# Row sums from ScalarE's accumulator, and gate work spread over four rounds, in a two-layer attention and expert kernel

## The chip, the cores and the metric

The kernel runs on one core of one Trainium2 chip. The metric is the device time of one execution in microseconds (us). Engines: TensorE (PE; its weight loads are PEld), VectorE (DVE), ScalarE (ACT), GpSimd (POOL) and SyncE (SP), each with an instruction stream of its own, synchronized by semaphores.

## What is computed

Two layers over x (16 batches, 128 rows, 128 columns, float32). Each layer adds a cross attention and a mixture of experts to x. The parts that matter here are the second attention and the first layer's gate:

```
x = x + attention_0(layernorm(x), ctx)
l = layernorm(x) @ gate_w.T                 # 8 experts
top_val, top_idx = top_k(l, 2);  w = softmax(top_val)
x = x + sum_e w_e * (layernorm(x) @ We[e])  # the two best experts of each row
q, k, v from layernorm(x) and ctx, 16 heads of 64
p     = softmax(q k / 8) over the first 124 context rows
p_ipa = softmax(q k / 8) over the last 4 context rows
x = x + ((p v + p_ipa v) @ Wo + ...)
x = x + experts_1(layernorm(x))             # 16 experts choose their rows
```

## The kernel before, in words

All engines run hand-written, software-pipelined rounds, one for each batch b. After the first attention's rounds (`round0`) come the second attention's (`round1`, b from -1 to 16), and then the second layer's experts. The work of one batch is spread over several rounds. In round b of `round1`:

- PE makes the scores of batch b (L1490, `scores`, two halves of 16 matmuls), transposes the powers of batch t = b - 1 (L1501, `turn`), makes queries (L1510), keys (L1518) and values (L1538) of batch f = b + 1, the outputs of t (L1531), the first layer's expert products of batch g = b + 4 (L1443, `ffn`, two halves in bank 7), and the projection of t (L1700).
- DVE, for each of four groups of four heads: `shifted` (L759 to L762) takes the maxima of the scores, `turned` (L770) copies transposed powers out of PSUM, `summed` (L776, L778) adds up the 124 powers of each head, in one reduction for four heads, and takes the reciprocal. It also does half of the scaling of the expert products (L732), the softmax over the last 4 context rows (`ipa_norm`, L783 to L787), the residual (L306), statistics (L310, L572, L575) and normalized inputs (L301).
- ACT: `powers` (L1130) makes the exponentials, one instruction for each head, 128x124, with the head's negated maximum as bias; `queries`, `outputs`, `values` and the key copy (L1137, L1143, L1148, L1237) bring results out of PSUM; `weighted` (L1092) scales four expert products.
- POOL: `norm` (L498) multiplies four heads' powers with the reciprocals, `experts_sum` (L481, L483) adds the eight scaled expert products of g, `rstds` (L432) gives the power -1/2 of variances.

The **gate work** is done for four batches at a time, j = 0 to 3 (group j is batches 4j to 4j + 3). Its parts are `head_input` (DVE, L698: four normalized inputs), `head_turn` (PE, L1431), `head_turned` (ACT, L1079), `head_logits` (PE, L1438, then three steps on DVE, L705 to L707), `head_powers` (ACT, L1084) and `head_weights` (DVE, nine steps, L713 to L725: ties and beats over all pairs of experts, 128x256 elements, the count, and the shares). Each of the twelve DVE steps adds one to the semaphore F.step, and DVE waits for it before the next; ACT's `weighted` waits for the twelfth of its group. `head_of(b)` says in which round a group is done: j = 1 in round -1, 2 in round 3, 3 in round 7. Groups 2 and 3 take their inputs at the ends of rounds 2 and 6 (`if b in (2, 6)`), and their weights at the ends of rounds 3 and 7, behind `ipa_norm` and ahead of the residual. Group 2 is first used by `weighted` in round 4, group 3 in round 8.

The order on each engine is the order of the calls in `round1`; nothing is reordered. In round b, PE waits for the residual of t - 1 (Z.x_new) before it writes bank 7 again, and for the first copied block of t (Z.p_sb) before the second half of the queries. The transposes of t wait for POOL's `norm` of t and for `ipa_norm`.

```
if j:
    head_turn(j, bank[7])
...
if there(g):
    if j:
        pe.wait_ge(F.step, HEAD_STEPS * j + 1)
    ffn(g, 0, bank[7])
```

## Time and profile before

| | |
|---|---|
| time, median of 3 runs | 526.05 us (525.59 to 528.3) |
| the profiled execution's own time | 526.27 us |
| its span, first to last instruction | 524.5 us |
| granted TensorE clock, mean | 0.998 of full |
| PE, PEld busy | 494.0, 380.1 us |
| DVE, ACT, POOL busy | 396.8, 271.6, 235.3 us |

A row of a timeline gives the start, the time until the last of its instructions ends, engine, line of the kernel, operation, out<-in, shapes and count (xN: so many instructions in one row); in brackets the idle time of the engine just before and who ended it. Instructions of one engine can overlap, so that a next row may start a little before the end of the one ahead. A row of the table by stretch gives the length and each engine's busy time in it.

### The profile page before, as it was taken

How to read it: one execution, taken by the hardware profiler on the slowest of the kernel's cores; microseconds unless marked ns; L12 is line 12 of the kernel's file. 1: busy time of each engine (PE TensorE's matmuls, PEld its weight loads, DVE VectorE, ACT ScalarE, POOL GpSimd, SP SyncE). 2: the span in 40 equal slices, each digit the busy share in tenths (PEclk: the TensorE clock that was granted, in tenths of full speed). 3: DMA queues.
4: the chain of work that ended last, by engine and by line, in shares of the span. 5: the costliest groups of instructions: out<-in, count | busy, mean ns of one | idle time of the engine just before them, and what ended most of it. 6: DMA issues, size and time to landing. Idle time of an engine off the chain costs nothing.

```text
span 524.5 us, 13371 instructions
## 1 busy us (share of the span) xinstructions
PE 494.0 (94%) x5109; PEld 380.1 (72%) x5113; DVE 396.8 (76%) x1064; ACT 271.6 (52%) x728; POOL 235.3 (45%) x331
## 2 busy tenths in 40 slices
PE   4799999999999998999989999999989999999996
PEld 3566666656667776777767777788757897799995
DVE  5888989766797889777897879778986678536553
ACT  3366565445666565564745575564663544513332
POOL 5845454044365542675245653533321890080540
PEclk9999999999999999999999999999999999999999
DMA  8900000000001110111000000022200300001001
GB/s 229 224 4 3 2 2 3 4 1 7 4 1 32 32 34 0 32 32 33 2 1 2 4 2 1 3 63 62 55 10 19 104 0 2 0 4 41 2 2 41
DMA packets 21872, 14.47 MB, mean 28 GB/s; under 512 B 5929, under 2 KB 21137, under 8 KB 21809
## 3 DMA queue, kind: packets, MB, share of 16 engines
q1 hardware_dynamic: 20704, 13.31, 9.7%
q8 instruction: 42, 0.69, 0.6%
q10 hardware_dynamic: 1104, 0.30, 0.3%
q14 instruction: 22, 0.17, 0.1%
HBM read 12.30 MB, written 1.05 MB: 25 GB/s over the span
## 4 chain that ended last, share of the span: by engine, by line
PE 74%; DVE 18%; issue 3%; ACT 2%; DMA 1%; POOL 1%; ACTq 0%; DVEq 0%; POOLq 0%
PE bank L1771 9%; PE bank L1780 5%; PE bank L1531 5%; PE bank L1443 5%; PE bank L1354 5%; PE bank L1538 4%; PE bank L1518 4%; PE bank L1700 4%; PE bank L1490 4%; PE bank L1510 4%; PE bank L1501 3%; PE bank L1787 3%; PE bank L1589 3%; PE bank L1339 3%; DVE negmax L760 2%
## 5 line engine op out<-in xcount | busy, mean ns | idle before, releaser
L498 POOL TENSOR_TENSOR work<-work,rsum 128x496 f32<-128x496 f32 x64 | 64.1, 1014 | 131.7 <-DVE rsum L778 131.7
L1130 ACT ACTIVATE work<-bank,negmax 128x124 f32<-128x124 f32 x256 | 72.5, 376 | 77.7 <-DVE ipa_s L762 77.7
L533 POOL TENSOR_SCALAR work<-work,slot 128x128 f32<-128x128 f32 x64 | 49.6, 792 | 48.3 <-DVE slot L853 29.4
L1771 PE MATMUL bank<-work 128*128 128x256 f32 x224 | 53.4, 381 | 0.0
L995 DVE SCALAR_TENSOR_TENSOR work<-work,bank 128x256 f32<-128x256 f32 x64 | 26.9, 420 | 33.0 <-ACT work L1282 32.8
L481 POOL TENSOR_TENSOR work<-work 128x512 f32<-128x512 f32 (+2 forms) x48 | 40.2, 838 | 12.1 <-DVE work L732 9.6
L1282 ACT ACTIVATE work<-bank 128x256 f32<-128x256 f32 x64 | 24.5, 383 | 40.6 <-PE bank L1771 29.1
L1771 PEld LDWEIGHTS bank<-work 128*128 128x128 f32 x224 | 40.3, 190 | 4.7 <-DVE work L998 0.2
L760 DVE TENSOR_REDUCE negmax<-bank 128x4 f32<-128x496 f32 x64 | 42.3, 661 | 0.0
L776 DVE TENSOR_REDUCE sums<-work 128x4 f32<-128x496 f32 x64 | 41.4, 647 | 0.5 <-ACT work L1130 0.5
L629 DVE TENSOR_REDUCE negmax<-bank 128x8 bf16<-128x1024 f32 x32 | 39.1, 1220 | 3.1 <-PE bank L1324 2.5
L432 POOL TENSOR_TENSOR rstd<-veps,minus_half 128x1 f32<-128x1 f32 (+3 forms) x28 | 21.0, 752 | 45.3 <-DVE veps L575 45.2
L1510 PE MATMUL bank<-xT,work 128*128 128x128 f32 x256 | 34.6, 279 | 7.0 <-DVE x_all L306 4.1
L770 DVE COPY work<-bank 128x512 f32<-128x512 f32 x60 | 40.7, 678 | 0.8 <-PE bank L1501 0.8
L1490 PEld LDWEIGHTS bank<-work 64*128 64x128 f32 x512 | 31.1, 187 | 13.9 <-issue 8.9
L1501 PE MATMUL bank<-ident,work 128*128 128x128 f32 x256 | 40.1, 279 | 0.3 <-DVE work L787 0.3
L1490 PE MATMUL bank<-work 64*128 64x128 f32 x512 | 37.2, 285 | 1.0 <-issue 1.0
L1510 PEld LDWEIGHTS bank<-xT,work 128*128 128x128 f32 x256 | 31.1, 192 | 9.4 <-issue 4.7
L1071 ACT ACTIVATE work<-bank 128x1024 f32<-128x1024 f32 x32 | 31.0, 1021 | 11.8 <-PE bank L1339 11.8
L1531 PEld LDWEIGHTS bank<-work 128*64 128x64 f32 x512 | 27.4, 136 | 13.3 <-issue 10.4
L1700 PEld LDWEIGHTS bank<-work 128*128 128x128 f32 x256 | 31.0, 191 | 7.4 <-issue 5.1
L1531 PE MATMUL bank<-work 128*64 128x128 f32 x512 | 35.0, 279 | 0.8 <-DVE work L770 0.6
(197 smaller groups left out, 1082.7 us busy)
## 6 DMA issues: line engine op xcount, KB each, us to landing
work<-in_L_ffn_w_dram SPq DMA_DIRECT2D x42, 128.0 KB, 2.4
x_all<-in_x_dram SPq DMA_DIRECT2D x4, 256.0 KB, 5.3
out_dram<-x_all SPq DMA_DIRECT2D x4, 256.0 KB, 2.5
ctx_all<-in_ctx_dram SPq DMA_DIRECT2D x4, 192.0 KB, 5.8
ctx_all<-in_L_ffn_w_dram SPq DMA_DIRECT2D x6, 128.0 KB, 2.3
work<-in_L_xattn_Wq_dram SPq DMA_DIRECT2D x1, 512.0 KB, 6.8
work<-in_L_xattn_Wo_dram SPq DMA_DIRECT2D x1, 512.0 KB, 9.1
work<-in_L_ffn_We_dram SPq DMA_DIRECT2D x1, 512.0 KB, 6.6
```

What stands on the lines that cost most here:

```text
L498: pool.tensor_tensor(part, part, rsum1[:, b % 2, CH * n:CH * n + CH].unsqueeze(2).broadcast_to((128, CH, ORG)), ALU.mult).then_inc(Z.norm, 1)
L533: ins = pool.tensor_scalar(ohw_of(e)[:, k, :], count[:, :], slot[:, h, 0, k, e % E1:e % E1 + 1], slot[:, h, 1, k, e % E1:e % E1 + 1], ALU. ...
L760: dve.tensor_reduce(negmax1[:, b % 2, part], got_s[:, :, 0:ORG], X, ALU.max, negate=True)
L770: dve.tensor_copy(p1T[:, CH * n:CH * n + CH, :], blocks(bank[(4, 6, 5, 4)[n]])).then_inc(Z.p_sb, 1)
L776: dve.tensor_reduce(sums1[:, b % 2, part], p1[:, b % 2, n, :, 0:ORG], X, ALU.add).then_inc(Z.sum, 1)
L1130: ins = act.activation(p1[:, b % 2, n, c, 0:ORG], blocks(bank[n])[:, c, 0:ORG], ACT.Exp, bias=negmax1[:, b % 2, CH * n + c:CH * n + c + 1])
L1490: mm = pe.matmul(blocks(bank[2 * half + odd])[:, c, :], q1T[rows, b % 2, CH * half + c, :], k1T[rows, b % 2, CH * half + c, :], start=True ...
L1501: mm = pe.transpose(blocks(bank[(4, 6, 5, 4)[n]])[:, c, :], p1[:, t % 2, n, c, :], ident[:, :])
L1510: mm = pe.matmul(blocks(bank[5 - n])[:, c, :], wq1[:, part], xT[:, f % 2, :], start=True, stop=True)
L1531: mm = pe.matmul(blocks(bank[5 - n])[D1 * odd:D1 * odd + D1, c, :], v1[:, t % 2, D1 * h:D1 * h + D1], p1T[:, CH * (2 * n + odd) + c, :], s ...
L1700: mm = pe.matmul(bank[7][:, 0:D], o1T[:, c, :], wo1[:, c, :], start=(c == 0), stop=(c == 7))
L1771: mm = pe.matmul(halves(bank[4 + c])[:, n, :], up_weights(e, n, c), xgT[e // E1][:, :, e % E1, :], start=True, stop=True)
```

## The change

ACT's exponentials get an accumulator output, which writes the sum of each head's 124 powers to `sums1`; DVE's reduction L776 and its semaphore go, and `summed` is the reciprocal alone. The gate work of groups 2 and 3 is moved: inputs are taken two at a time at the ends of rounds -1 and 0 (group 2) and 3 and 4 (group 3); transposes and logits are in rounds 1 and 5; the nine steps of the weights are split into `head_ties` (two steps, rounds 2 and 6), `head_beats` (three, rounds 3 and 7) and `head_shares` (four, rounds 4 and 8). Ties and beats stand in front of the third `shifted`, shares in front of `ffn_statistics`. ACT's `head_turned` stands ahead of the first `powers` of its round instead of behind it. PE waits for the input copy xT of batch b + 1 before the gate's transposes.

```diff
--- before.py
+++ after.py
@@ -253,7 +253,7 @@
 
         W = named(sem, "w", "turned downT alpha ctx made taken added")
         Z = named(sem, "z", "xn xb tr xT q q_sb k0 k1 k0_sb k1_sb ki v v_sb vi0 vi1 score ipa_max maxed ipa_exp ipa_step ipa_p "
-                            "exp sum rsum norm turned p_sb p_odd o o_sb proj x_new stats")
+                            "exp rsum norm turned p_sb p_odd o o_sb proj x_new stats")
 
         R = named(sem, "r", "wide count tok picks xn tr xT hid th h logit max ex step topx top turned slot")
         G = named(sem, "g", "told oh got xg")
@@ -295,7 +295,7 @@
 
         def head_of(b):
 
-            return (b + 5) // 4 if (b + 5) % 4 == 0 and b <= 7 else None
+            return {-1: 1, 1: 2, 5: 3}.get(b)
 
         def dve_xn(dve, Z, b, u):
             dve.tensor_scalar(xn[:, u, :], x_all[:, b, :], mv[:, b, 0:1], rstd[:, b, :],
@@ -706,16 +706,23 @@
                 step(dve.tensor_reduce(top0[:, :], lg[:, :, :], X, ALU.max))
                 step(dve.tensor_tensor(ew[:, :, :], lg[:, :, :], top0[:, :].unsqueeze(2).broadcast_to(each), ALU.subtract))
 
-            def head_weights(j):
-
-                mine = lg[:, :, :].unsqueeze(3).broadcast_to(pairs)
-                other = lg[:, :, :].unsqueeze(2).broadcast_to(pairs)
+            mine = lg[:, :, :].unsqueeze(3).broadcast_to(pairs)
+            other = lg[:, :, :].unsqueeze(2).broadcast_to(pairs)
+
+            def head_ties():
+
                 step(dve.tensor_tensor(tie[:, :, :, :], other, mine, ALU.is_ge))
                 step(dve.tensor_tensor(tie[:, :, :, :], tie[:, :, :, :], lower[:, :, :].unsqueeze(1).broadcast_to(pairs),
                                        ALU.mult))
+
+            def head_beats():
+
                 step(dve.tensor_tensor(beat[:, :, :, :], other, mine, ALU.is_gt))
                 step(dve.tensor_tensor(beat[:, :, :, :], beat[:, :, :, :], tie[:, :, :, :], ALU.max))
                 step(dve.tensor_reduce(nbeat[:, :, :], beat[:, :, :, :], X, ALU.add))
+
+            def head_shares(j):
+
                 dve.wait_ge(F.ex, j + 1)
                 step(dve.scalar_tensor_tensor(ew[:, :, :], nbeat[:, :, :], 1.5, ew[:, :, :], ALU.is_lt, ALU.mult))
                 step(dve.tensor_reduce(wsum[:, :], ew[:, :, :], X, ALU.add))
@@ -723,6 +730,12 @@
                 to = ffn_w[:, 4 * (j % 2):4 * (j % 2) + 4, :]
                 after(dve, F.ys0, 4 * (j - 1))
                 step(dve.tensor_tensor(to, ew[:, :, :], wsum[:, :].unsqueeze(2).broadcast_to(each), ALU.mult))
+
+            def head_weights(j):
+
+                head_ties()
+                head_beats()
+                head_shares(j)
 
             def weighted(g, got_y):
 
@@ -773,8 +786,6 @@
 
                 dve.wait_ge(Z.exp, CH * b + n + 1)
                 part = slice(CH * n, CH * n + CH)
-                dve.tensor_reduce(sums1[:, b % 2, part], p1[:, b % 2, n, :, 0:ORG], X, ALU.add).then_inc(Z.sum, 1)
-                dve.wait_ge(Z.sum, CH * b + n + 1)
                 dve.reciprocal(rsum1[:, b % 2, part], sums1[:, b % 2, part]).then_inc(Z.rsum, 1)
 
             def ipa_norm(b):
@@ -883,8 +894,14 @@
                     hidden(1)
                 if b == 14:
                     eight(0, 1)
+                if b in (4, 8):
+                    head_shares((b + 4) // 4)
                 if there(b + 3) and b >= 0:
                     ffn_statistics(b + 3)
+                if b in (2, 6):
+                    head_ties()
+                if b in (3, 7):
+                    head_beats()
                 if there(b):
                     shifted(b, 2)
                 if b == 12:
@@ -921,8 +938,8 @@
                     summed(b, 2)
                     summed(b, 3)
                     ipa_norm(b)
-                if head_of(b):
-                    head_weights(head_of(b))
+                if b == -1:
+                    head_weights(1)
                 if there(b + 3) and b < 0:
                     ffn_statistics(b + 3)
                 if b == 9:
@@ -953,8 +970,10 @@
                     slot_weights(0)
                 if b == 15:
                     rstd_at["half", 2] = variances(Z.stats, B - 1, 12, B - 1)
-                if b in (2, 6):
-                    head_input((b + 6) // 4)
+                if b in (-1, 3):
+                    head_input((b + 9) // 4, 0, 2)
+                if b in (0, 4):
+                    head_input((b + 8) // 4, 2, 4)
                 if there(b + 3):
                     xn1_of(b + 3)
                 if b == -1:
@@ -1127,8 +1146,9 @@
 
                 act.wait_ge(Z.maxed, CH * b + n + 1)
                 for c in range(CH):
+                    h = CH * n + c
                     ins = act.activation(p1[:, b % 2, n, c, 0:ORG], blocks(bank[n])[:, c, 0:ORG], ACT.Exp,
-                                         bias=negmax1[:, b % 2, CH * n + c:CH * n + c + 1])
+                                         bias=negmax1[:, b % 2, h:h + 1], accum_out=sums1[:, b % 2, h:h + 1])
                 ins.then_inc(Z.exp, 1)
 
             def queries(f, n):
@@ -1182,10 +1202,10 @@
 
             def round1(b):
                 f, t, g = b + 1, b - 1, b + 4
+                if head_of(b):
+                    head_turned(head_of(b), bank[7])
                 if there(b):
                     powers(b, 0)
-                if head_of(b):
-                    head_turned(head_of(b), bank[7])
                 if b == 12:
                     route_turned(0)
                 if b == 13:
@@ -1602,6 +1622,7 @@
                     gather(4)
                 after(pe, Z.x_new, t)
                 if j:
+                    after(pe, Z.xT, b + 2)
                     head_turn(j, bank[7])
                 if b == 12:
                     route_turn(0, bank[7])
```

## Rows read from the trace of the kernel before

**Rows 1.** Part 1 of the page: busy time and share of each engine

```profile
PE 494.0 (94%) x5109; PEld 380.1 (72%) x5113; DVE 396.8 (76%) x1064; ACT 271.6 (52%) x728; POOL 235.3 (45%) x331
```

**Rows 2.** Stretches: length, then PE, PEld, DVE, ACT, POOL busy, clock; rounds 1, 3, 4, 5

```profile
145.57:162.05 16.48, 15.86 (x138) 12.25 (x138) 13.37 (x37) 10.30 (x31) 11.31 (x16) 1.00 0.09 26
...
177.62:196.28 18.66, 17.36 (x151) 13.56 (x150) 16.90 (x44) 10.51 (x31) 8.13 (x11) 1.00 0.09 24
196.28:214.80 18.52, 16.07 (x138) 12.27 (x138) 15.16 (x43) 9.69 (x29) 8.20 (x13) 1.00 0.09 24
214.80:230.37 15.57, 15.57 (x138) 12.22 (x137) 12.10 (x35) 9.69 (x29) 7.95 (x12) 1.00 0.10 28
```

**Rows 3.** Timeline of PE, rounds 3 and 4

```profile
179.93 0.63 PE L1431 MATMUL bank<-ident,work 128*128 128x128 f32 x4 [0.56 <-DVE work L698]
...
182.62 1.06 PE L1438 MATMUL bank<-work 128*128 128x8 f32 x8 [0.74 <-ACT work L1079]
...
200.06 1.16 PE L1510 MATMUL bank<-xT,work 128*128 128x128 f32 x8 [2.03 <-DVE x_all L306]
```

**Rows 4.** Timeline of DVE, rounds 2 to 4

```profile
178.27 1.51 DVE L698 TENSOR_SCALAR work<-x_all,mv,rstd 128x128 f32<-128x128 f32 x4
...
193.98 1.25 DVE L713 TENSOR_TENSOR work<-work 128x256 f32<-128x256 f32 x1
195.26 1.37 DVE L714 TENSOR_TENSOR work<-work,lower 128x256 f32<-128x256 f32 x1
...
199.71 0.29 DVE L306 TENSOR_TENSOR x_all<-bank,x_all 128x128 f32<-128x128 f32 x1
```

**Rows 5.** Timeline of DVE, round -1

```profile
128.67 0.42 DVE L714 TENSOR_TENSOR work<-work,lower 128x256 f32<-128x256 f32 x1
...
132.74 1.28 DVE L301 TENSOR_SCALAR xn<-x_all,mv,rstd 128x128 f32<-128x128 f32 x1 [0.66 <-POOL rstd L432]
```

**Rows 6.** Timeline of DVE, round 5

```profile
218.69 0.66 DVE L776 TENSOR_REDUCE sums<-work 128x4 f32<-128x496 f32 x1
...
220.75 0.17 DVE L759 TENSOR_REDUCE ipa_max<-bank 128x4 f32<-128x16 f32 x1 [0.62 <-PE bank L1490]
```

**Rows 7.** Timeline of ACT, round 3: the smallest activation

```profile
190.02 0.24 ACT L1084 ACTIVATE work<-work 128x32 f32<-128x32 f32 x1
```

**Rows 8.** All instructions of line L1130: duration ns min/median/max, first and last start

```profile
L1130 ACT ACTIVATE work<-bank,negmax x256: 354/365/474, 137.3 to 388.0; 128x124 f32<-128x124 f32 x128
```

**Rows 9.** Timeline of ACT, round 5

```profile
216.86 1.13 ACT L1130 ACTIVATE work<-bank,negmax 128x124 f32<-128x124 f32 x4 [3.15 <-DVE ipa_s L762]
...
219.80 1.21 ACT L1092 ACTIVATE work<-bank,work 128x128 f32<-128x128 f32 x4
221.62 1.13 ACT L1130 ACTIVATE work<-bank,negmax 128x124 f32<-128x124 f32 x4 [0.61 <-DVE ipa_s L762]
222.97 1.13 ACT L1130 ACTIVATE work<-bank,negmax 128x124 f32<-128x124 f32 x4 [0.21 <-DVE ipa_s L762]
...
224.57 0.60 ACT L1143 ACTIVATE work<-bank 128x512 f32<-128x512 f32 x1 [0.34 <-PE bank L1531]
```

**Rows 10.** Timeline of PE, round 5

```profile
222.48 1.02 PE L1443 MATMUL bank<-work 128*128 128x512 f32 x2
...
226.56 1.12 PE L1538 MATMUL bank<-work,cT_all 96*124 96x512 f32 x2
```

**Rows 11.** Timelines of PE and ACT, round 0

```profile
141.55 1.12 PE L1443 MATMUL bank<-work 128*128 128x512 f32 x2
...
140.29 1.21 ACT L1092 ACTIVATE work<-bank,work 128x128 f32<-128x128 f32 x4
141.31 2.22 ACT L1130 ACTIVATE work<-bank,negmax 128x124 f32<-128x124 f32 x8
```

**Rows 12.** Timeline of PE, rounds 14 and 15

```profile
372.17 1.09 PE L1531 MATMUL bank<-work 128*64 128x128 f32 x16 [0.35 <-DVE work L770]
...
386.50 1.13 PE L1589 MATMUL bank<-work 128*128 128x512 f32 x2 [0.87 <-DVE work L861]
```

## The prediction

> **What bounds the kernel now.** I read the engines' shares first [rows 1]: TensorE (PE) is busy 94% of the span, VectorE (DVE) 76%, ScalarE (ACT) 52%. So time can only come out of places where PE stands still, or in by making it stand. The table by stretch [rows 2] cuts the second attention at the starts of PE's score matmuls. The ordinary round (214.80 to 230.37) takes 15.57 us and PE is busy for all of it: nothing that DVE or ACT saves there moves the time. Round 3 takes 18.66 and round 4 18.52; rounds 7 and 8 repeat them to the hundredth. Those four are 3.09 + 2.95 + 3.09 + 2.95 = 12.08 us above the ordinary round, and that is the sum in play. Round 1 is 0.91 above.
>
> Where the 12.08 goes is in PE's timeline [rows 3]. In round 3 PE waits 0.56 for the four gate inputs, then 0.74 for ACT's copy of their transposes; the gate's own matmuls are four in 0.63 and eight in 1.06, so 0.11 each and 0.2 to fill: twelve and one filling are about 1.4 that PE has to do. This, with the waits and their restarts, is the excess. In round 4 PE waits 2.03 for the residual. DVE's timeline [rows 4] says why: the nine steps of the gate weights run from 193.98 to 199.71 ahead of the residual, 5.7 us, while PE had ended that round's projection at about 196.3. The two-input steps are slow there: L713 took 1.25 and L714 1.37, beside GpSimd's expert sums. The same L714 took 0.42 in round -1, while GpSimd was idle [rows 5].
>
> **The change, part by part.** *Sums.* 64 reductions on DVE go, four a round, 0.66 each [rows 6], spaced 0.68 with the wait: 2.7 us of DVE a round. In an ordinary round they are hidden: DVE waits for PE 0.62 before L759 even so. What is left on DVE is the reciprocal, which now waits for ACT.
>
> *The accumulator on ACT.* The trace has no activation with an accumulator. I count it as one more small instruction behind each of the 16 activations of a round, r each. Nearest row: the 128x32 activation at 0.24 [rows 7]. Four exponentials of 0.365 (the median [rows 8]) take 1.13 together [rows 9], so neighbours overlap by (4 x 0.365 - 1.13) / 3 = 0.11. If the read overlaps like its neighbours, r is 0.24 - 0.11 = 0.13, or 0.09 with so few elements; if it neither overlaps nor lets the next start, r is 0.24 + 0.11 = 0.35. Below zero is excluded, as work is only added. I take 0.13, since every back-to-back pair in the rows overlaps, and keep 0.09 and 0.35 for the range.
>
> The Trainium skill ("ScalarE: Activation LUTs", section on what ACT_TABLE_LOAD costs) gives an activation with immediates 186 ns + 0.833 per element and an overlap of 93: one element would then add 94 ns, an estimate by that page, and the sum below would come out about 0.6 us lower. The page does not price the accumulator's read, and by its own figures an exponential of 124 elements would be spaced 290 ns, where the rows give 255; so I stay with the rows.
>
> What ACT can bear in an ordinary round [rows 9, 10]: the scaled copies L1092 end at 221.01 and PE needs them at 222.48, 1.47 later, with 8 reads ahead: r up to 0.18. The output copy L1143 ends at 225.17 and PE's L1538 starts at 226.56, 1.39 later, with 16 reads ahead, and ACT idled 0.61 + 0.21 + 0.34 before, plus 3 x 0.11 of overlap: 2.88 / 16, again 0.18. So at 0.13 the read is hidden in every ordinary round and costs nothing; above 0.18 it costs up to 16 x (r - 0.18) a round. This is the one threshold of the case.
>
> *Where ACT has no cover: round 0* [rows 11]. PE's second expert matmul starts at 141.55, as ACT's copies end (141.50), so 8 reads delay it by 1.0; the last powers, end 143.5, go back by 16 reads, and with them the key copy behind them, which PE's last value matmul of the round needs. 2.1 us on ACT bound it above, the 1.0 below; I take +1.5 for round 0, in the middle. Round 1's 0.9 of excess came from DVE's reductions ahead of the softmax's rest; they are gone: -0.9.
>
> *The gate inputs.* Four L698 in one place become two and two, at the ends of rounds -1 and 0, and 3 and 4. In round -1 the pair falls into the 0.66 that DVE waits for GpSimd's power before L301 [rows 5]: nothing. Round 0 has no residual to end with. At the end of round 3 it puts 2 x 0.38 [rows 4] ahead of the shift and copy of round 4, for which PE's second query half waits; how much PE has in hand there no row says, so 0 to 0.75, and I take +0.2, since in the ordinary round PE does not wait for that copy at all. At the end of round 4 the next round begins with the gate's matmuls, which cover it.
>
> *Gate matmuls.* They move from rounds 3 and 7 to 1 and 5. PE keeps 2 x 1.4 = +2.8. The inputs are a round old, so the 0.56 goes; ACT now copies the transposes ahead of the first powers, where it idled 3.15 [rows 9], so the 0.74 goes. The powers start about 0.5 later, behind which PE has 1.4 more work of its own.
>
> *Gate weights.* Nine steps, 5.7 us, come out of the end of rounds 3 and 7. Two go in front of the third shift of rounds 2 and 6, three into 3 and 7, four into 4 and 8. Uncontended they take 0.9, 1.3 and 1.1 (0.42 to 0.43 a wide step [rows 5]); GpSimd's first normalization, about 1 us, may hit the first of them: 1.3, 1.7 and 1.1. The place has 0.62 of wait plus the 0.68 of the reduction that left, 1.3. What runs over (0.4) delays the third copy. In round 5 the shift begins at 220.75 [rows 6] and with its copy takes about 1.4, to 222.2; PE comes to the outputs that need it behind L1443, about 223.4 [rows 10]: 1.2 in hand, so 0.4 is hidden. The shares in round 4 end about when ACT reaches the scaled copies that wait for them. So these steps cost nothing as long as the reduction is gone too.
>
> *The added wait* on xT ahead of the transposes is for a copy made a round before: nothing. No DMA moves; SP's queue is untouched.
>
> *Rounds 14 and 15.* DVE holds PE there: 0.35 before L1531 and 0.87 before a gather [rows 12]. The reduction just ahead leaves: -0.5 in round 14. In round 15 DVE gains about 1 but ACT's gathered copies come later by some of the reads: -0.5.
>
> **Sum:** -12.08 + 2.8 + 0.2 + 1.5 - 0.9 - 0.5 - 0.5 = -9.5 us. The profiled execution took 526.27 (span 524.5), 0.2 above the median of 526.05; it becomes 516.8, and the median 516.5. A measurement of this kernel can tell about 0.5% (2.6 us) from no change.
>
> **Rivals.** *A, ACT becomes the bound.* The read is slow, r above 0.18. Place: PE's L1538 waits for the output copy in every round from 1 to 14. Price: at 0.25, 16 x 0.07 = 1.1 a round, 14 rounds, +15.7, less the 9.5, about 532; at 0.35 about 555. It decides from r = 0.22, where 14 x 0.64 = 9.0 eats the gain; between 0.18 and 0.22 it gives 517 to 526. For it: nothing in the trace shows that the read overlaps. Against it: all neighbours do. This is the case on the slower side.
> *B, the gate steps meet GpSimd in their new places.* As slow as in [rows 4], the ties take 2.66 instead of 1.3; the third shift is then 1.4 late, the copy behind it misses PE's outputs by 0.2, and ACT's powers, as late, their output copy by up to 0.6, in rounds 2, 3, 6 and 7: +0.8 to +2.4, with round 15 giving nothing, 518 to 520. For it: L714 did take 1.37. Against: the normalization is one instruction of 1 us, the expert sums three.
> *C, the accumulator does not give what it is there for,* and only the spreading pays: ordinary rounds hide it, and ACT's later results take back what DVE frees in rounds 1, 14 and 15. -12.08 + 2.8 + 0.2 + 1.5 = -7.6, 518.5. For it: [rows 2], where PE has no gap in an ordinary round. Against: the waits of [rows 12] end with DVE, not with ACT.
>
> **How the numbers follow.** Forecast 0.72 (512.5 to 518.2, r 0.09 to 0.18; the lower end: 0.5 more in round 0, 0.2 in round 4, 0.5 in round 15 and up to 2.7 where DVE, freed of 2.7 a round, stops holding PE in a way I do not see). B 0.10, C 0.05. A 0.13: 0.02 for an end below 523.4, 0.04 within 0.5%, 0.07 slower. The range 512.5 to 521 takes in the forecast, B and C and leaves out A's larger part. Faster by over 0.5%: 0.89; within: 0.04; slower: 0.07.
>
> **What would show it.** Rounds 3, 4, 7 and 8 at 15.6 to 15.8 us, rounds 1 and 5 at about 17.0, round 0 longer by 1 to 2; no PE wait for the residual in round 4; L1092 followed by powers without a gap; the spacing of four accumulating exponentials at about 1.5 to 1.7 us instead of 1.13. I am wrong if that group takes over 1.85 (A: then PE waits for ACT's L1143 in each round), if PE waits for DVE's third copy (B), or if L713 and L714 stay over 1 us.

## The result, and the profile after

The changed kernel takes 518.79 us (median of four runs, 517.55 to 519.62) where the kernel before, timed beside it, took 526.95 (525.59 to 528.3): a ratio of 0.984, 95% interval 0.981 to 0.987, so 8.2 us less. The forecast was 516.5, with 512.5 to 521. The profiled executions are 8.0 apart (518.3 with a span of 516.6, against 526.27 with 524.5).

Part 1 of the page, and the head of its part 4 (the chain that ended last), of the kernel after:

```profile
PE 494.2 (96%) x5113; PEld 381.7 (74%) x5113; DVE 355.0 (69%) x1000; ACT 291.0 (56%) x984; POOL 234.5 (45%) x331
...
PE 85%; DVE 8%; ACT 2%; issue 2%; DMA 1%; ACTq 1%; POOL 1%; DVEq 0%; POOLq 0%
```

Against [rows 1], DVE lost 41.8 us of busy time and 64 instructions. ACT gained 19.4 us and 256 instructions. PE's work is the same. What shrank is the time in which PE stood still. DVE held 18% of the chain before and holds 8% now.

The table by stretch of the kernel after (length; PE, PEld, DVE, ACT, POOL busy; granted clock; DMA share, GB/s), rounds 0, 1, 3, 4 and 5; rounds 1, 3, 4, 5 answer to [rows 2]:

```profile
135.34:147.56 12.22, 11.85 (x73) 8.46 (x73) 6.80 (x25) 9.13 (x42) 4.57 (x8) 0.86 0.01 1
147.56:165.37 17.81, 17.18 (x150) 13.61 (x150) 12.66 (x35) 12.24 (x48) 10.79 (x14) 1.00 0.08 24
...
180.94:196.52 15.58, 15.58 (x139) 12.23 (x138) 11.20 (x34) 10.92 (x45) 7.57 (x12) 1.00 0.10 28
196.52:212.57 16.05, 15.80 (x138) 12.25 (x137) 11.23 (x37) 10.82 (x45) 8.42 (x12) 1.00 0.10 28
212.57:229.48 16.91, 16.91 (x151) 13.54 (x150) 11.28 (x36) 11.53 (x47) 8.01 (x12) 1.00 0.09 26
```

Round 3 has become an ordinary round. Round 5 carries the gate's matmuls, and PE is busy for all of it. Rounds 1 and 4 still hold waits of PE. The length of every round, from one start of PE's score matmuls to the next, in the kernels that the text speaks of (us; of the rounds not shown, 2, 6 and 9 are 15.57 or 15.58 and 13 is 16.50 or within 0.01 of it in all of these):

| round | 0 | 1 | 3 | 4 | 5 | 7 | 8 | 10 | 11 | 12 | 14 |
|---|---|---|---|---|---|---|---|---|---|---|---|
| before | 10.25 | 16.48 | 18.66 | 18.52 | 15.57 | 18.65 | 18.53 | 16.09 | 16.77 | 16.77 | 14.37 |
| after | 12.22 | 17.81 | 15.58 | 16.05 | 16.91 | 15.57 | 15.58 | 15.95 | 16.55 | 16.91 | 13.78 |
| after, third profile (e11) | 11.42 | 17.14 | 15.57 | 16.05 | 16.91 | 15.57 | 15.57 | 15.95 | 16.55 | 16.90 | 13.78 |
| e1, accumulator alone | 11.42 | 15.57 | 18.80 | 16.01 | 15.57 | 18.80 | 16.00 | 15.96 | 16.53 | 16.90 | 13.78 |
| e2, spreading alone | 11.85 | 19.54 | 15.97 | 16.43 | 17.98 | 15.99 | 15.58 | 16.09 | 16.78 | 16.77 | 14.36 |
| e4, inputs early | 11.42 | 16.90 | 15.57 | 15.57 | 16.91 | 15.57 | 15.58 | 15.95 | 16.55 | 16.90 | 13.78 |
| e9, all early | 12.23 | 16.90 | 15.58 | 15.57 | 16.91 | 15.57 | 15.58 | 15.57 | 15.58 | 15.90 | 13.78 |

After against before: rounds 3, 4, 7 and 8 give 3.08 + 2.47 + 3.08 + 2.95 = 11.58. Rounds 0, 1 and 5 take back 1.97 + 1.33 + 1.34 = 4.64. Rounds 10 to 12 give 0.22, round 14 gives 0.59 and round 15 0.22. That is 7.97 of the 8.0.

The clock matters for rounds 0 and 1. In the profiles of after, e2 and e9 the granted TensorE clock fell for a stretch of round 0 (its mean there is 0.86 in after), in those of before, e1, e4 and e11 it did not. So after is best read against e9, and e11 against before, e1 and e4. At full clock round 0 is 1.17 longer than before and round 1 0.66; with the fall they are 1.97 and 1.33 longer. The stages ahead of round 0 end anywhere from 133.7 to 137.3 us in the 13 profiles of this case, so one span against another is a coarser measure than the rounds.

Five lines of the timeline of PE after. They are the waits that are left in rounds 1 and 4, and three in round 15:

```profile
149.94 0.63 PE L1451 MATMUL bank<-ident,work 128*128 128x128 f32 x4 [0.63 <-DVE work L698]
...
199.84 1.13 PE L1530 MATMUL bank<-xT,work 128*128 128x128 f32 x8 [0.24 <-DVE work L783]
...
375.73 1.12 PE L1609 MATMUL bank<-work 128*128 128x512 f32 x2 [0.19 <-DVE work L872]
377.21 0.38 PE L1601 MATMUL bank<-work,b_pick 128*128 128x512 bf16 x1 [0.36 <-ACT work L1173]
...
378.43 1.12 PE L1609 MATMUL bank<-work 128*128 128x512 f32 x2 [0.41 <-DVE work L872]
```

PE's wait of 2.03 for the residual [rows 3] is gone. In round 4 it now waits 0.24 for DVE's first copy (L783, L770 before), behind a pair of gate inputs that took 0.93. In round 15 its two waits for the one-hot rows shrank from 0.45 (at 383.74 in the trace before) and 0.87 [rows 12] to 0.19 and 0.41, but its bf16 matmul L1601 waits 0.36 for ACT's copy of transposed powers (L1173, L1153 before), which stands behind accumulating exponentials and frees the bank.

The timeline of ACT after in round 0, the exponentials with their accumulator:

```profile
137.37 0.36 ACT L1150 ACTIVATE work<-bank,negmax 128x124 f32<-128x124 f32 x1 [4.44 <-DVE ipa_s L775]
137.64 0.19 ACT L1150 ACTIVATION_READ_ACCUMULATOR work<-bank,negmax 128x1 f32 x1
137.73 0.35 ACT L1150 ACTIVATE work<-bank,negmax 128x124 f32<-128x124 f32 x1
137.97 0.20 ACT L1150 ACTIVATION_READ_ACCUMULATOR work<-bank,negmax 128x1 f32 x1
138.07 0.36 ACT L1150 ACTIVATE work<-bank,negmax 128x124 f32<-128x124 f32 x1
```

The accumulator's read is an instruction of its own behind every exponential, here 0.2 long. It overlaps both neighbours: exponentials start 0.34 to 0.36 apart, where 1.13 for four [rows 9] made it 0.255. So r is about 0.09.

The timeline of DVE after, the gate steps in rounds 2 and 3:

```profile
169.92 0.87 DVE L714 TENSOR_TENSOR work<-work 128x256 f32<-128x256 f32 x1
170.83 0.42 DVE L715 TENSOR_TENSOR work<-work,lower 128x256 f32<-128x256 f32 x1
...
185.50 0.87 DVE L720 TENSOR_TENSOR work<-work 128x256 f32<-128x256 f32 x1
186.40 0.43 DVE L721 TENSOR_TENSOR work<-work 128x256 f32<-128x256 f32 x1
186.86 0.42 DVE L722 TENSOR_REDUCE work<-work 128x32 f32<-128x256 f32 x1
```

Ties take 1.3 and beats 1.7. The first step of each is slow, beside a normalization of GpSimd's (169.50 to 170.51, and 185.08 to 186.09); the other three are not.

### The profile page after: what moved, and what is told of

Same layout as the page of the kernel before. It is cut to its first block, busy times and chain, and to the rows that moved or that the text cites. A ratio compares the mean times of both kernels' runs of the same rounds, so it can differ in the third digit from the quotient of the medians.

```text
span 516.6 us, 13574 instructions
## 1 busy us (share of the span) xinstructions
PE 494.2 (96%) x5113; PEld 381.7 (74%) x5113; DVE 355.0 (69%) x1000; ACT 291.0 (56%) x984; POOL 234.5 (45%) x331
## 3 DMA queue, kind: packets, MB, share of 16 engines
HBM read 12.30 MB, written 1.05 MB: 26 GB/s over the span
## 4 chain that ended last, share of the span: by engine, by line
PE 85%; DVE 8%; ACT 2%; issue 2%; DMA 1%; ACTq 1%; POOL 1%; DVEq 0%; POOLq 0%
PE bank L1792 9%; PE bank L1551 6%; PE bank L1558 6%; PE bank L1721 6%; PE bank L1538 5%; PE bank L1510 5%; PE bank L1463 5%; PE bank L1530 5%; PE bank L1801 5%; PE bank L1521 5%; PE bank L1374 5%; PE bank L1808 3%; PE bank L1609 3%; PE bank L1359 3%; PE bank L1344 1%
## 5 line engine op out<-in xcount | busy, mean ns | idle before, releaser
L1150 ACT ACTIVATE work<-bank,negmax 128x124 f32<-128x124 f32 x256 | 89.9, 383 | 52.6 <-DVE ipa_s L775 52.5
L1150 ACT ACTIVATION_READ_ACCUMULATOR work<-bank,negmax 128x1 f32 x256 | 58.0, 226 | 0.0
L306 DVE TENSOR_TENSOR x_all<-bank,x_all 128x128 f32<-128x128 f32 x16 | 4.7, 292 | 59.5 <-PE bank L1721 57.1
L783 DVE COPY work<-bank 128x512 f32<-128x512 f32 x60 | 40.9, 681 | 0.8 <-PE bank L1521 0.8
L1530 PE MATMUL bank<-xT,work 128*128 128x128 f32 x256 | 35.9, 287 | 1.4 <-DVE work L783 1.3
L1538 PE MATMUL bank<-cT_all,work 96*128 96x124 f32 x256 | 35.2, 281 | 0.3 <-DVE work L919 0.3
```

The costliest lines, as they stand in the source:

```text
L783: dve.tensor_copy(p1T[:, CH * n:CH * n + CH, :], blocks(bank[(4, 6, 5, 4)[n]])).then_inc(Z.p_sb, 1)
L1150: ins = act.activation(p1[:, b % 2, n, c, 0:ORG], blocks(bank[n])[:, c, 0:ORG], ACT.Exp, bias=negmax1[:, b % 2, h:h + 1], accum_out=sums1[ ...
L1530: mm = pe.matmul(blocks(bank[5 - n])[:, c, :], wq1[:, part], xT[:, f % 2, :], start=True, stop=True)
L1538: mm = pe.matmul(bank[6][:, ORG * c:ORG * c + ORG], wk1[0:C, part], cT_all[:, f, 0:ORG], start=True, stop=True)
```

## The experiments

**The two halves, the change again, and the gate inputs moved.** All four were timed beside the kernel before (median 526.85).

*e1* is the kernel before with the accumulator instead of the reduction; the gate work stays where it was.

```diff
-                dve.tensor_reduce(sums1[:, b % 2, part], p1[:, b % 2, n, :, 0:ORG], X, ALU.add).then_inc(Z.sum, 1)
-                dve.wait_ge(Z.sum, CH * b + n + 1)
...
-                                         bias=negmax1[:, b % 2, CH * n + c:CH * n + c + 1])
+                                         bias=negmax1[:, b % 2, h:h + 1], accum_out=sums1[:, b % 2, h:h + 1])
```

> The kernel before with the accumulator alone; the gate work stays where it was. Theory S (the steps of the prediction, with the 0.09 us for a read that the changed kernel's profile shows): round 0 longer by 1.4, the 0.9 of excess in round 1 gone, rounds 3 and 7 shorter by about 2.0 each, because three reductions of 0.68 no longer stand ahead of the nine gate steps, round 14 by 0.6, round 15 by 0.2: -4.3 us in all, near 522. Rival N (the accumulator gives nothing, the spreading alone pays): no faster than before, 526 to 528, with the cost of round 0 visible. Rival D (the two parts are worth something only together): within 1 us of before.

It took 520.85, ratio 0.989 (0.986 to 0.992), 6.0 less. The timeline of its DVE in round 3:

```profile
190.71 0.42 DVE L713 TENSOR_TENSOR work<-work 128x256 f32<-128x256 f32 x1
...
195.91 0.29 DVE L306 TENSOR_TENSOR x_all<-bank,x_all 128x128 f32<-128x128 f32 x1
```

Round 3 starts at 176.39 here. The nine steps begin 14.3 us into it instead of 16.4 [rows 2, 4], since three reductions are gone between DVE's last wait for PE and them (3 x 0.68 = 2.0), and take 5.2 instead of 5.7. The residual comes 2.6 earlier, so round 4 falls from 18.52 to 16.01 although nothing of the gate was moved. Round 8 does the same. Rounds 3 and 7, which I had expected 2.0 shorter each, are 0.14 longer: the gain comes one round later, where PE had waited for the residual. Round 1 loses its 0.91, round 14 loses 0.59, and round 0 pays 1.17. DVE was worth more off the ordinary round than my sum gave it, because its saving and the spreading buy the same wait.

*e2* is the change without the accumulator: the reduction and its wait are back, the gate work is spread.

```diff
+                dve.tensor_reduce(sums1[:, b % 2, part], p1[:, b % 2, n, :, 0:ORG], X, ALU.add).then_inc(Z.sum, 1)
+                dve.wait_ge(Z.sum, CH * b + n + 1)
...
-                                         bias=negmax1[:, b % 2, h:h + 1], accum_out=sums1[:, b % 2, h:h + 1])
+                                         bias=negmax1[:, b % 2, CH * n + c:CH * n + c + 1])
```

> The changed kernel with the reductions back on VectorE and no accumulator. Theory S: rounds 3, 7 and 8 at 15.6, since the third copy has 1.2 us in hand and the gate steps overrun the wait of 0.62 by 0.7 to 1.1; rounds 5 at 16.9; round 0 back at 10.3; round 1 worse than in the changed kernel, as its reductions and two gate inputs both stand before the first shift: about 19; rounds 14 and 15 as before. In all -12.1 + 2.8 + 1.5 + 0.5 = -7.3, near 519.3, so most of the gain. Rival D (the steps find room only where the reduction left): the third shift is late beyond what is in hand, 0.5 to 1 us in each of rounds 2, 3, 4, 6, 7 and 8: 523 to 525.

It took 522.64, ratio 0.992 (0.988 to 0.995), 4.2 less. The timeline of its PE, rounds 1 and 4:

```profile
150.25 0.63 PE L1452 MATMUL bank<-ident,work 128*128 128x128 f32 x4 [1.57 <-DVE work L698]
...
154.51 1.13 PE L1464 MATMUL bank<-work 128*128 128x512 f32 x2 [0.52 <-DVE work L705]
...
201.63 1.13 PE L1531 MATMUL bank<-xT,work 128*128 128x128 f32 x8 [0.62 <-DVE work L783]
```

With the reductions back, DVE is late in most of the places that the gate work went to. PE waits 1.57 + 0.52 in round 1 and 0.62 in round 4; rounds 3 and 7 are 0.4 over the ordinary one, and round 5 takes 17.98. Rounds 2, 6 and 8 are at 15.58: ties and shares are free there even so. The beats, the inputs and the gate's own rounds were cheap only because the reduction had left. I had put the price of its return too low: 519.3 was expected, and 522.64 lies close to rival D's 523 to 525, though not in all of the rounds that D named: it is in 1, 3, 4, 5 and 7.

*e3* is the changed kernel again.

> The changed kernel itself, as the measure beside the others of this call. Both theories: 518 to 519, -8 us. If the slow stretch of the clock in round 0 belongs to the change (TensorE starved by ScalarE ahead of it), it is there again, with round 0 at 12.2; if it is chance, round 0 comes at about 11.7.

It took 517.54, ratio 0.982 (0.979 to 0.985), 9.3 less. The halves give 6.0 and 4.2. Their sum is 10.2, and the whole gives 8.2 to 9.3, which these intervals alone do not keep apart. By the rounds, they buy the same wait twice and help each other elsewhere: rounds 4 and 8 give 5.04 in e1, 5.04 in e2 and 5.42 in both together, while rounds 1 and 5 are 5.5 above the kernel before in e2, 0.9 below it in e1, and 2.7 above it with both.

*e4* is the change with the gate inputs moved ahead: in rounds 3 and 4 ahead of the residual, and in round 0 ahead of the third shift. The pair of round -1 stays.

```diff
+                if b == 0:
+                    head_input(2, 2, 4)
                 if b in (2, 6):
                     head_ties()
...
+                if b in (3, 4):
+                    head_input(3, 2 * (b - 3), 2 * (b - 2))
                 if there(t):
                     dve.wait_ge(Z.proj, t + 1)
...
-                if b in (-1, 3):
-                    head_input((b + 9) // 4, 0, 2)
-                if b in (0, 4):
-                    head_input((b + 8) // 4, 2, 4)
+                if b == -1:
+                    head_input(2, 0, 2)
```

> The changed kernel with the second pair of group 2's gate inputs in round 0's wait for the second scores, and both pairs of group 3 ahead of the residual, where VectorE waits over 3 us, in place of behind it. Theory S: TensorE's waits of 0.63 in round 1 and the 0.48 of round 4 are the inputs' place: round 1 at about 17.0, round 4 at 15.6, -1.2 us against the changed kernel. Rival (those waits come from the copies and GpSimd's contention, wherever the inputs stand): less than 0.4.

It took 516.83, ratio 0.981 (0.978 to 0.984), 0.7 below e3, too little for the intervals to part. The traces do part them. Three stretches of its table, rounds 0, 1 and 4:

```profile
135.16:146.58 11.42, 10.22 (x73) 7.00 (x74) 7.70 (x27) 8.94 (x42) 4.46 (x7) 1.00 0.01 2
146.58:163.48 16.90, 16.90 (x150) 13.55 (x149) 10.26 (x32) 12.15 (x48) 10.90 (x15) 1.00 0.09 25
...
194.63:210.20 15.57, 15.57 (x138) 12.22 (x137) 11.07 (x37) 10.85 (x45) 8.33 (x12) 1.00 0.10 27
```

Rounds 1 and 4 have no wait of PE left, and round 0 is no longer than in e1 and e11. So the excess of rounds 1 and 4 in the changed kernel is the place of the gate inputs and nothing else. In round 1 that excess depends on the clock in round 0: at full clock it is 17.14 - 16.90 = 0.24 (e11 against e4), with the fall 17.81 - 16.90 = 0.91 (after against e9). And 16.90 - 15.57 = 1.33 is what the gate's twelve matmuls cost.

**The price of a small ACT instruction, round 0, and the order on ACT.** Each of these four ran once, and so did the kernel before beside them (526.68).

*e5* is the change with a copy of one column behind each exponential, 16 a round.

```diff
                                          bias=negmax1[:, b % 2, h:h + 1], accum_out=sums1[:, b % 2, h:h + 1])
+                    act.activation(spare_a[:, 0 + h:0 + h + 1], negmax1[:, b % 2, h:h + 1], ACT.Copy)
```

> The changed kernel with one more activation of one column (a copy of one number into unused memory) behind each exponential, so that the cost r of each rises from 0.09 to about 0.18, the threshold that the prediction worked out. Theory S: rounds 2, 3, 6, 7 and 9 stay at 15.6 to 15.7; round 0 longer by another 1.4; in all +2 against the changed kernel. Rival L (ScalarE has no room left at 0.09 already): every round longer by 16 x 0.09 = 1.4, +20 in all.

*e6* has two such copies behind each exponential.

```diff
+                    act.activation(spare_a[:, 0 + h:0 + h + 1], negmax1[:, b % 2, h:h + 1], ACT.Copy)
+                    act.activation(spare_a[:, 16 + h:16 + h + 1], negmax1[:, b % 2, h:h + 1], ACT.Copy)
```

> The same with two such activations, r about 0.27. Theory S: above the threshold of 0.18 each ordinary round is longer by 16 x 0.09 = 1.4 us, TensorE waiting for ScalarE's output copy or scaled copies: rounds 2, 3, 6, 7 at about 17.0, +19 in all, near 537. Rival M (ScalarE is idle 4.7 us of an ordinary round, so 16 x 0.18 = 2.9 more fits): rounds stay at 15.6, +3 in all.

e5 took 523.66 and e6 543.82, about 5 and 25 us above the changed kernel, where +2 and +19 had been expected. The timeline of ACT in e5, round 2, and the stretch of that kernel's round 2:

```profile
170.27 0.36 ACT L1151 ACTIVATE work<-bank,negmax 128x124 f32<-128x124 f32 x1
170.52 0.20 ACT L1151 ACTIVATION_READ_ACCUMULATOR work<-bank,negmax 128x1 f32 x1
170.61 0.20 ACT L1153 ACTIVATE spare_a<-negmax 128x1 f32<-128x1 f32 x1
170.70 0.36 ACT L1151 ACTIVATE work<-bank,negmax 128x124 f32<-128x124 f32 x1
```

```profile
167.33:183.05 15.72, 15.72 (x138) 12.25 (x137) 11.19 (x33) 12.05 (x61) 7.92 (x12) 1.00 0.09 27
```

The stretch of round 2 of e6, and two lines of its PE:

```profile
169.28:186.41 17.13, 16.10 (x139) 12.27 (x138) 11.12 (x33) 13.53 (x77) 8.29 (x13) 1.00 0.09 25
```

```profile
177.74 1.13 PE L1466 MATMUL bank<-work 128*128 128x512 f32 x2 [0.32 <-ACT work L1112]
...
182.60 1.12 PE L1561 MATMUL bank<-work,cT_all 96*124 96x512 f32 x2 [0.59 <-ACT work L1166]
```

The extra copy adds 0.09 to the spacing (0.43), so e5 stands for r = 0.18 and e6 for r = 0.27. At 0.18 the ordinary round has just begun to grow, 15.57 to 15.72. At 0.27 it is 17.13, 1.56 longer, where 16 x (0.27 - 0.18) gives 1.4, and PE waits in the two places that the prediction named: the expert matmul for the scaled copies, and the value matmul (L1561, L1538 before) for the output copy. Taken back from these two, the threshold is 0.18 - 0.15 / 16 = 0.17 and 0.27 - 1.56 / 16 = 0.17, where the prediction worked out 0.18. At r = 0.09 the changed kernel stands well below it. Rival M, by which ACT's idle time of a whole round could be filled, is refuted. The expectation's totals came out too low because it counted mostly the ordinary rounds: in e5 round 0 grows by 1.43 at full clock (12.85 against e11's 11.42), as said, but rounds 12 and 14 by 0.37 and 0.73 as well.

*e7* is the change with the reductions back on DVE in round 0 alone.

```diff
+                if b == 0:
+                    dve.tensor_reduce(sums1[:, b % 2, part], p1[:, b % 2, n, :, 0:ORG], X, ALU.add).then_inc(Z.sum, 1)
+                    dve.wait_ge(Z.sum, CH * b + n + 1)
...
+                    total = dict(accum_out=sums1[:, b % 2, h:h + 1]) if b else {}
```

> The changed kernel, but in round 0 the sums are VectorE's reductions again and the exponentials have no accumulator. Theory S: round 0 back to 10.3 (11.0 if the clock is low for a stretch in it), so 16 reads cost 1.2 to 1.4 there; round 1 longer by 1.5 to 2, since three reductions again stand ahead of the softmax's rest and the two gate inputs. Rival (the longer round 0 is the clock's alone): round 0 stays over 11.4.

It took 519.16. Round 0 is 11.84 (12.22 after, both with the stretch of low clock told of below) and round 1 is 18.85 (17.81). The gate inputs start 0.8 later (148.30 instead of 147.52), so 0.4 is won and 1.0 lost. The expectation failed here: with a low stretch it said 11.0 for round 0, and 11.84 lies where the rival (the clock's alone) had put it. But the rival does not hold either, since round 0 is 1.17 longer than before in e1, e4 and e11, where the clock stayed up. The two causes overlap: with the fall PE is busy through much of the time in which it would wait for ACT, so the reads add 12.22 - 11.84 = 0.4 there and 1.17 at full clock.

*e8* puts ACT's copy of the gate's transposes back behind the first exponentials.

```diff
-                if head_of(b):
-                    head_turned(head_of(b), bank[7])
                 if there(b):
                     powers(b, 0)
+                if head_of(b):
+                    head_turned(head_of(b), bank[7])
```

> The changed kernel with ScalarE's copy of the gate's transposes behind the first powers again, as before. Theory S: TensorE waits for it in rounds 1 and 5; four exponentials now take 1.4 and not 1.0, so the wait is 0.74 + 0.35 less the 0.9 of queries that TensorE has before it in both kernels: rounds 1 and 5 longer by 0.7 to 1.1 each, +1.4 to 2.2 in all. Rival (no difference, TensorE has other work there): under 0.3.

It took 519.83. A single execution does not part that from the changed kernel (in it the stages ahead of round 0 were 1.4 shorter than in the one shown above), but the rounds do: round 1 is 19.50 and round 5 is 18.27. Two lines of its PE:

```profile
151.95 1.06 PE L1458 MATMUL bank<-work 128*128 128x8 f32 x8 [1.51 <-ACT work L1098]
...
217.41 1.06 PE L1458 MATMUL bank<-work 128*128 128x8 f32 x8 [1.10 <-ACT work L1098]
```

The order on ACT alone is worth 19.50 - 17.81 = 1.7 and 18.27 - 16.91 = 1.4. Without the two lines that change places, 3.1 us of the gain by the rounds would be lost.

**What is left** (kernel before: median 526.89).

*e9* is e4 with every step that stood between the residual and the next shift in rounds 9 to 14 put ahead of the residual as well: variances, the normalized halves and the slot weights.

```diff
-                if there(t):
-                    dve.wait_ge(Z.proj, t + 1)
-                    dve.wait_ge(Z.xb, t + 1)
-                    dve_residual(dve, Z, t, bank[7][:, 0:D])
-                    dve_stats(dve, Z, t)
                 if b == 9:
                     rstd_at["half", 0] = variances(Z.stats, HB, 0, HB)
                 if b in (10, 11):
                     normalize(xn_half[0], 4 * (b - 10), 4 * (b - 9), rstd_at["half", 0], R.xn)
...
                 if b == 14:
                     slot_weights(0)
+                if there(t):
+                    dve.wait_ge(Z.proj, t + 1)
+                    dve.wait_ge(Z.xb, t + 1)
+                    dve_residual(dve, Z, t, bank[7][:, 0:D])
+                    dve_stats(dve, Z, t)
```

> The kernel with early inputs, and besides the second layer's normalized rows (rounds 10 and 11), its variances (rounds 9 and 13) and slot weights (round 14) ahead of the residual, where VectorE waits 3 to 4.5 us, in place of behind it. Theory S: what stands between residual and first copy is TensorE's wait at the start of the next round: round 10 at 15.6 (-0.4), 11 at 15.6 (-1.0), 12 at 16.0 (-0.9), round 15 by about 0.5; with the inputs' 1.2 it is 3.5 to 4 below the changed kernel, 514 to 515. Rival (GpSimd's work at the end of a round slows these instructions so much that the residual is late): no gain over the kernel with early inputs.

*e10* is e9 with the first two of round 0's four sums on DVE.

```diff
+                if b == 0 and n < 2:
+                    dve.tensor_reduce(sums1[:, b % 2, part], p1[:, b % 2, n, :, 0:ORG], X, ALU.add).then_inc(Z.sum, 1)
+                    dve.wait_ge(Z.sum, n + 1)
...
+                    total = {} if b == 0 and n < 2 else dict(accum_out=sums1[:, b % 2, h:h + 1])
```

> The same, but in round 0 the sums of the first two groups of heads are VectorE's reductions, so that only 8 reads stand on ScalarE's path, none of them ahead of the scaled copies. Theory S: round 0 shorter by 0.7 to 1.2 (near 10.5), round 1 unchanged at 16.9: another -1. Rival (VectorE's two reductions come ahead of the softmax's rest and round 1 gives it back): the same as the kernel without it.

*e11* is the changed kernel once more, timed beside these two.

> The changed kernel once more, beside the two above: -8 to -9 us against before, 518. All theories the same; its trace shows whether the slow stretch of the clock comes again in round 0.

e9 took 514.45, ratio 0.977 (0.973 to 0.980); e10 513.78, 0.975 (0.971 to 0.978); e11 518.08, 0.983 (0.980 to 0.986). So e9 is 3.6 us faster than the changed kernel and beats both kernels. Three stretches of e9, rounds 10 to 12:

```profile
290.17:305.74 15.57, 15.57 (x138) 12.22 (x137) 12.00 (x35) 10.85 (x45) 9.55 (x13) 1.00 0.02 4
305.74:321.32 15.58, 15.58 (x139) 12.22 (x138) 12.00 (x35) 10.85 (x45) 7.93 (x12) 1.00 0.01 2
321.32:337.22 15.90, 15.61 (x144) 12.81 (x144) 9.43 (x31) 11.30 (x44) 6.55 (x11) 1.00 0.10 28
```

and what stood in those places in the kernel after, from its PE's timeline:

```profile
311.54 0.46 PE L1530 MATMUL bank<-xT,work 128*128 128x128 f32 x2 [0.73 <-DVE work L783]
328.10 1.13 PE L1530 MATMUL bank<-xT,work 128*128 128x128 f32 x8 [0.32 <-DVE work L783]
329.42 1.12 PE L1576 MATMUL bank<-work 128*128 128x512 f32 x2 [0.19 <-ACT work L1184]
333.84 1.09 PE L1551 MATMUL bank<-work 128*64 128x128 f32 x16 [0.29 <-DVE work L783]
```

Rounds 10, 11 and 12 lose 0.38, 0.97 and 1.01; rounds 1 and 4 lose 0.91 and 0.48. Round 15, expected about 0.5 shorter, is 14.63 against 14.84; its waits for ACT and for DVE's one-hot rows (0.37 and 0.41) are still there. Of the four waits only the last is still there in e9 (0.29 at 329.88). e10's split of round 0 did not show the 0.7 to 1.2 that was expected: its round 0 is 12.19 against 12.23, both with the fall of the clock, and the intervals of the two overlap. Whether it pays at full clock is not settled.

## Why the prediction was right, and by how much it missed

The forecast case happened by its mechanism: 516.5 was said and 518.8 measured. The number alone would not have told, since it lies nearer to rival C's 518.5 and inside rival B's 518 to 520; the rounds and e1 decide. The sum said -9.5 and the profiled pair gave -8.0. By the prediction's own steps:

**Sums and accumulator.** Removing the reductions costs nothing and frees 2.7 us of DVE a round; e1 shows it. It is worth more than the 0.9, 0.5 and 0.5 that the sum booked for it, as it also shortens the wait of rounds 4 and 8. The read costs r = 0.09, which was the lower bound; "I take 0.13, since every back-to-back pair in the rows overlaps" was too careful. The estimate that I worked out from the Trainium skill ("ScalarE: Activation LUTs", section on what ACT_TABLE_LOAD costs), 94 ns for one element, agrees with the 0.09 measured here for the read and with the 0.09 that e5's one-column copy added.

**The threshold** of 0.18 is confirmed by e5 and e6, which give 0.17. Rival A's mechanism exists, but r was half of what it needs.

**Rounds 3, 4, 7 and 8** gave 11.58 of 12.08. Three of them are at 15.57 or 15.58, as said. Round 4 (16.05, where 15.6 to 15.8 was to show it) kept 0.48 where I had taken 0.2. That term, "how much PE has in hand there no row says, so 0 to 0.75", was sized low inside its bounds; e4 takes the inputs away from there and the round is 15.57.

**Gate matmuls** cost 1.34 each, forecast 1.4 (twelve at 0.11 and 0.2 to fill, its own terms, are 1.5). The order on ACT was counted as removing 0.74 a round, but e8 puts it at 1.4 to 1.7. I had taken the wait of the old round 3. With the accumulator the four exponentials hold ACT for 1.37 ahead of the copy (215.38 to 216.75 in e8's round 5) instead of 1.00 (180.96 to 181.96 before), and 0.74 + 0.37 is the 1.10 that PE waits there.

**Gate inputs at the end of round 0** is the step that failed: "Round 0 has no residual to end with", with nothing in the sum. Round 1 was forecast at 16.48 - 0.9 + 1.4 = 16.98 and took 17.81 with the fall of the clock, 17.14 without. The DVE timeline after, rounds -1 and 0 (the same pair of instructions twice), and GpSimd's beside the second:

```profile
131.97 0.60 DVE L698 TENSOR_SCALAR work<-x_all,mv,rstd 128x128 f32<-128x128 f32 x2
...
147.52 2.27 DVE L698 TENSOR_SCALAR work<-x_all,mv,rstd 128x128 f32<-128x128 f32 x2
```

```profile
146.51 1.98 POOL L498 TENSOR_TENSOR work<-work,rsum 128x496 f32<-128x496 f32 x2
...
148.45 2.61 POOL L481 TENSOR_TENSOR work<-work 128x512 f32<-128x512 f32 x3
```

In round -1 GpSimd had only a one-column power beside it, and the pair took 0.60, hidden as forecast. At the end of round 0 it runs beside the normalizations and the expert sums, takes 2.27, and PE's transposes wait 0.63 for it. In e11 the pair and the transposes behind it are:

```profile
147.20 2.01 DVE L698 TENSOR_SCALAR work<-x_all,mv,rstd 128x128 f32<-128x128 f32 x2
...
149.65 0.60 PE L1451 MATMUL bank<-ident,work 128*128 128x128 f32 x4
```

There the pair is slow too, but it starts 0.86 ahead of round 1 instead of 0.04, and PE does not wait for it; round 1 exceeds e4's by only the 0.24. The step ahead of the pair (L798) starts 0.07 ahead of a normalization in e11 and takes 0.23; in after it starts 0.05 behind one and takes 1.04. It takes 0.23 in all three profiles at full clock with these reads (e1, e4, e11) and 1.03 or 1.04 in four with the fall (after, e3, e8, e9), so the late pair goes with the fall. The price of 0.38 an instruction came from [rows 4], another place. The Trainium skill ("SBUF — State Buffer", section "Who interferes with whom") says that a tensor_scalar can enter a mode that takes the port pair shared with GpSimd, and that of two instructions which want it, the later is blocked until the earlier ends. The trace agrees with the blocking, as the single durations of that line in the two places show (ns, min/median/max, first and last start); the mode itself no row shows:

```profile
L698 DVE TENSOR_SCALAR work<-x_all,mv,rstd x2: 344/345/346, 132.0 to 132.2; 128x128 f32<-128x128 f32 x2
...
L698 DVE TENSOR_SCALAR work<-x_all,mv,rstd x2: 1050/1176/1302, 147.5 to 148.5; 128x128 f32<-128x128 f32 x2
```

The first of the slow two starts at 147.52, 0.04 behind a normalization of 1.01, and ends 0.08 after it. The second starts at 148.50, 0.05 behind an expert sum of 1.26, and ends 0.09 after it.

I had used that caution for L713 and L714 (Rival B) and not for L698.

**Round 0** was forecast at +1.5. It is +1.17 in every profile of these reads at full clock (e1, e4, e11) and +1.97 in the one above, where the clock fell. The reads of ACT were thus priced a little high. PE ends the round waiting for the key copy, 0.41 in e11, as the prediction said.

**Rounds 14 and 15:** -0.59 and -0.22, forecast -0.5 each. In round 15 PE's two waits for DVE lost 0.26 and 0.46, and a new one for ACT's copy of transposed powers took 0.36 back. That ACT would give some of it back was in the step ("ACT's gathered copies come later by some of the reads"), but it was another of its copies, and more of it. Rounds 10 to 12 gave 0.22 that were not in the sum.

So the 1.5 between sum and trace are: round 1, 0.83; round 0, 0.47; round 4, 0.28; round 15, 0.28; less 0.22 for rounds 10 to 12 and small ones. But of rounds 0 and 1, 1.5 together go with the fallen clock, which no term of the sum had: the two take 30.03 here and 28.56 in e11. At full clock, by e11's rounds 0 to 15 against those before, the change gives 9.5, the sum itself. That its single terms miss by up to 0.33 each way and cancel is luck, and e11's span is 8.1 shorter than before and not 9.5 because the stages ahead of its round 0 took 1.3 more.

**The rivals.** B did not happen: ties and beats took 1.3 and 1.7 as forecast, and none of rounds 2, 3, 6 and 7 is over 15.58. C is refuted by e1: the accumulator alone gives 6.0, and it is the spreading alone that gives the less, 4.2. Behind C stood my own sum, which booked rounds 4 and 8 wholly to the spreading.

**One sign was half wrong:** "L1092 followed by powers without a gap". It holds in rounds 2, 4, 6, 8 and 9. In rounds 3 and 7 ACT waits 0.31 for the third shift, ahead of which the beats now stand. In round 5 it waits 0.57 (0.61 before), since PE reaches the second scores later by the gate's matmuls. And four accumulating exponentials with their reads take 1.49, where 1.5 to 1.7 was said.

## What to carry to other kernels

A saving on an engine that is idle in the ordinary round still counts where its work piles up ahead of something that TensorE needs; look for the rounds in which that engine is named as the releaser, and expect two edits that shorten the same wait not to add up. Before adding an instruction to an engine, work out from one ordinary round how much each can grow before the next engine waits (here 0.18 us a head; two experiments put it at 0.17). Compare rounds only with rounds of the same granted clock: here the fall hides two thirds of one cost and enlarges another. Price a moved instruction by the row of what runs beside it in its new place, and put steps that nobody waits for ahead of the residual that starts the next round, not behind it.

## What the runs showed of the hardware

**The accumulator's read** is an instruction of its own, 0.19 to 0.32 long in the kernel after (median 0.22), and costs 0.09 of spacing, as much as a one-column copy. ACT's busy time grew by 19.4 us for 256 of them, 0.076 each, although their durations add up to 58.

**TensorE's clock.** Two profiles of the same kernel, after and e11, in PE's rows of round 0:

```profile
135.34 1.16 PE L1510 MATMUL bank<-work 64*128 64x128 f32 x16 [1.06 <-issue]
136.43 3.65 PE L1530 MATMUL bank<-xT,work 128*128 128x128 f32 x16
```

```profile
136.64 1.16 PE L1510 MATMUL bank<-work 64*128 64x128 f32 x16 [1.05 <-issue]
137.73 2.05 PE L1530 MATMUL bank<-xT,work 128*128 128x128 f32 x16
```

PE had stood for 1.06 and 1.05 us before. In the first the granted clock then fell to its 1.2 GHz level (0.86 as the mean of the round), and 16 matmuls took 3.65 instead of 2.05; in the second it stayed at 2.4 GHz. The fall stands in this place in 8 of the 13 profiles of this case (after, e2, e3, e6 to e10). It costs 0.8 in round 0 of the changed kernel, and 1.6 where DVE does that round's sums (11.85 in e2 and 11.84 in e7, with the fall, against 10.25 before, without). In the changed kernel another 0.7 goes in round 1, where the late DVE work meets the gate's transposes; in e9, whose inputs are early, round 1 stays at 16.90 even so. It occurred in neither of the two kernels without a pair of gate inputs in round -1 (before and e1), and in 8 of the 11 profiles with one. Two are too few to say that the change makes it likelier, and that was not settled.
